# The expert stage of a one-core conv, attention and mixture-of-experts block: 39 groups of 256 slots against 32 groups of 256 and seven of 128

## The reference

```python
x = x + conv(group_norm(x))                 # 16 Fourier modes
t = tokens(x)
t = t + attention(layer_norm(t))            # causal within each sequence of 256
# mixture of experts, on layer_norm(t):
router_probs = softmax(flat_x @ router_w)   # 8 experts
topk_w, topk_idx = top_k(router_probs, 2)   # then normalised to sum 1
for e in range(8):
    h = gelu(flat_x @ w_fc[e])              # 256 -> 1024
    out = out + combine[:, e:e+1] * (h @ w_proj[e])   # 1024 -> 256
```

## Time and profile before

| | |
|---|---|
| median of 3 runs | 723.77 us (722.03 to 724.03) |
| the profiled execution | 726.27 us |
| its span, first to last instruction | 724.5 us |
| mean granted TensorE clock | 0.964 of full |
| busy: PE, DVE, ACT, POOL | 647.4, 516.5, 413.7, 429.6 us |
| instructions | 16522 |

### The profile page before, as it was taken

How to read it: one execution, slowest core, us unless ns; L and a number is a source line. 1 busy time by engine, 2 the same in 40 slices (tenths; PEclk the granted TensorE clock), 3 DMA queues, 4 the chain that set the end, 5 groups by cost and what they waited for, 6 DMA issues and landing times. The chain is left out here.

```text
span 724.5 us, 16522 instructions
## 1 busy us (share of the span) xinstructions
PE 647.4 (89%) x5010; PEld 624.2 (86%) x5010; DVE 516.5 (71%) x1217; ACT 413.7 (57%) x703; POOL 429.6 (59%) x340
## 2 busy tenths in 40 slices
PE   0496999999940699999999999999999999999993
PEld 0385888888840599999999999999999999999993
DVE  8764577777764577787878777877787777777761
ACT  1804777766520556566666656565656565756550
POOL 5002326777666256766666666767676767676763
PEclk9999999999975799999999999999999999999998
DMA  8805752222323454433131313222222222232312
GB/s 343 273 0 186 276 179 74 92 90 97 106 105 113 136 162 146 96 108 59 29 59 31 57 31 57 41 47 45 43 49 39 51 37 52 36 53 35 57 19 29
DMA packets 39486, 64.13 MB, mean 89 GB/s; under 512 B 3808, under 2 KB 34848, under 8 KB 38304
## 3 DMA queue, kind: packets, MB, share of 16 engines
q0 software_dynamic: 14304, 18.92, 14.7%
q1 hardware_dynamic: 14816, 34.55, 13.5%
q10 hardware_dynamic: 10336, 10.31, 5.6%
HBM read 37.96 MB, written 25.81 MB: 88 GB/s over the span
## 5 line engine op out<-in xcount | busy, mean ns | idle before, releaser
L574 POOL TENSOR_TENSOR pj_lo<-w_ffn,pj_hi 128x1024 fp32r<-128x1024 f32 x78 | 189.1, 2425 | 122.8 <-ACT pj_hi L615 106.3
L1167 DVE TENSOR_TENSOR fc_lo<-w_ffn,fc_hi 128x1024 fp32r<-128x1024 f32 x78 | 116.1, 1527 | 86.2 <-ACT fc_hi L615 86.2
L564 POOL DMA_INDIRECT out<-y,add_id x78 | 121.9, 1563 | 45.1 <-issue 43.7
L615 ACT ACTIVATE pj_hi<-w_ffn 128x1024 fp32r x78 | 82.7, 1060 | 94.9 <-PE psO L1464 89.3
L615 ACT ACTIVATE fc_hi<-w_ffn 128x1024 fp32r x78 | 78.3, 1051 | 43.4 <-issue 43.4
L1464 PE MATMUL psP<-pj_hi,h_hi 128*128 128x256 f32 x312 | 91.5, 293 | 0.2 <-DVE h_lo L1167 0.2
L1464 PE MATMUL psP<-pj_hi,h_lo 128*128 128x256 f32 x312 | 88.5, 284 | 0.0
L1464 PE MATMUL psO<-pj_hi,h_lo 128*128 128x256 f32 x312 | 88.3, 283 | 0.0
L1464 PE MATMUL psO<-pj_lo,h_hi 128*128 128x256 f32 x312 | 88.3, 283 | 0.0
L1464 PE MATMUL psP<-pj_lo,h_hi 128*128 128x256 f32 x312 | 88.3, 283 | 0.0
L1464 PE MATMUL psO<-pj_hi,h_hi 128*128 128x256 f32 x312 | 88.1, 282 | 0.0
(11 more groups left out here) (252 smaller groups left out, 1639.4 us busy)
## 6 DMA issues: line engine op xcount, KB each, us to landing
w_ffn<-in_w_ffn SPq DMA_DIRECT2D x8, 2048.0 KB, 8.2
xg<-slots ACTq DMA_DIRECT2D x38, 265.0 KB
xc<-in_x_ch SPq DMA_DIRECT2D x4, 1024.0 KB, 8.9
out<-x SPq DMA_DIRECT2D x16, 256.0 KB
x<-in_x_tok SPq DMA_DIRECT2D x1, 3072.0 KB, 25.2
slots<-fill SPq DMA_DIRECT2D x9, 265.0 KB, 2.8
out<-y,add_id POOLq DMA_INDIRECT x78, 3.9
w_in<-in_w_in SPq DMA_DIRECT2D x1, 1024.0 KB, 13.7
```

Of the source, the lines that this page charges most:

```text
L564: nc.gpsimd.indirect_dma_start(out_d, bass.IndirectOffsetOnAxis(ap=add_id[:, s:s + 1], axis=0), y[:, s, :], None, compute_op=ALU.add).then ...
L574: nc.gpsimd.tensor_tensor(pj_lo[:, 4 * a:4 * a + 4, :], w_ffn[:, bass.ds(e, 1), (2 + a) * DFF:(3 + a) * DFF].rearrange("p a (c d) -> p (a ...
L615: nc.scalar.activation(out, src, ACT.Copy, **kw).then_inc(done, 1)
L1167: v.tensor_tensor(out, whole, upper.bitcast(F32), ALU.subtract).then_inc(done, 1)
```

## The change

The groups are now of two sizes, 32 of 256 slots and seven of 128. In units of 128 slots the stage handles 2 x 32 + 7 = 71 where it handled 2 x 39 = 78. The number of groups stays 39.

- **The plan.** DVE gives each expert as many full groups as its count of picks divided by 256, rounded (the last one rounded up), 32 at most, and what is left of each goes to groups of 128. `plan_halves` works the latter out: 30 more DVE instructions in a chain of their own (`half_step`), placed after the planning chain and ahead of `after_attention`.
- **The order.** `PARTS` gives the sizes: six full groups, then three turns of a loop of ten positions (128, 256, 256, 256, 256, twice), then 128, 256, 256. The groups of 128 stand at positions 6, 11, 16, 21, 26, 31 and 36. All engines, POOL too, run through `run_groups`.
- **A group of 128.** `up` keeps its 48 matmuls with 128 moving columns; `down` has 24 with 256 columns; two transposes; the GELUs, casts and subtractions of hidden values have half the columns; one output and one indirect DMA. The splits of the weights (`fc_hi`, `fc_lo`, `pj_hi`, `pj_lo`) stay whole.
- **Two buffers.** `y` and `add_id` are double. `outputs(g)` waits for the adds of group g-2; `add(g)` copies the numbers first and waits for the adds of g-1 after that.
- Small tiles (`numbers`, `counts`, `past`, `plan`) move to other places in SBUF, and a helper `planned` has each engine wait for the second plan at position 4.

The core of the diff:

```diff
-GROUPS = (TOK * PICKS - E) // GS + E
+UNIT = GS // 2
+UNITS = (TOK * PICKS - E) // UNIT + E
+FULL = TOK * PICKS // GS
+HALVES = UNITS - 2 * FULL
+GROUPS = FULL + HALVES
+assert HALVES >= E - 1
+
+HEAD, ROUNDS = 6, 3
+ROUND = (1, 2, 2, 2, 2) * 2
+PARTS = (2,) * HEAD + ROUND * ROUNDS + (1, 2, 2)
+assert PARTS.count(2) == FULL and PARTS.count(1) == HALVES
...
+def group_of(n, turn=None):
+
+    parts = PARTS[n]
+    at = PARTS[:n].count(2) if parts == 2 else FULL + PARTS[:n].count(1)
+    added, added_last = (16 * sum(PARTS[:max(m, 0)]) for m in (n, n - 1))
+    if turn is None:
+        return Group(n, at, parts, added, added_last)
+    step = 16 * sum(ROUND)
+    return Group(turn * len(ROUND) + n, turn * ROUND.count(parts) + at, parts, turn * step + added, turn * step + added_last)
...
-        add_id = place("always", "add_id", [P, 2], I32)
+        add_id = [place("always", f"add_id{n}", [P, 2], I32) for n in range(2)]
...
-        y = ff("y", [P, 2, D])
+        y = [ff(f"y{n}", [P, 2, D]) for n in range(2)]
...
+        def planned(eng, g):
+
+            if isinstance(g.n, int) and g.n == HEAD - 2:
+                eng.wait_ge(halves_ready, 1)
+
         def load_group(eng, g):
-            at_row = eng.value_load(table[0:1, 1, bass.ds(g, 1)], min_val=0, max_val=IDLE_ROW)
-            eng.dma_start(xg[:, :, :], slots_d[bass.ds(at_row, GS)].rearrange("(s p) r -> p s r", p=P)).then_inc(xg_loaded, 16)
+            at_row = eng.value_load(table[0:1, 1, bass.ds(g.at, 1)], min_val=0, max_val=IDLE_ROW)
+            eng.dma_start(xg[:, 0:g.parts, :],
+                          slots_d[bass.ds(at_row, g.parts * P)].rearrange("(s p) r -> p s r", p=P)).then_inc(xg_loaded, 16)
...
+        def hidden_in(g, c):
+
+            return banks[c][:, :].rearrange("p (f n) -> p f n", f=2)[:, :, 0:g.parts * P]
 
         def run_groups(eng, body):
 
-            body(0, 0)
-            pairs = (GROUPS - 2) // 2
-            with eng.Fori(0, pairs) as i:
-                body(i * 2 + 1, 1)
-                body(i * 2 + 2, 0)
-            for g in range(1 + 2 * pairs, GROUPS):
-                body(g, g % 2)
+            def run(n, turn=None):
+
+                before, here, after, second = (
+                    group_of(m, turn) if turn is not None or 0 <= m < GROUPS else None for m in (n - 1, n, n + 1, n + 2))
+                body(before, here, after, second, n % 2)
+
+            for n in range(HEAD):
+                run(n)
...
+            for n in range(HEAD + len(ROUND) * ROUNDS, GROUPS):
+                run(n)
...
-            def add(g):
-                if later(g):
-                    pool.wait_ge(y_added, g * 32)
-                pool.wait_ge(meta_read, g * 2 + 2)
+            def add(g, par):
+                pool.wait_ge(meta_read, g.n * 2 + 2)
                 gate()
-                nc.gpsimd.tensor_copy(add_id[:, :], slot_id[:, bass.ds(g, 1), :]).then_inc(id_ready, 1)
-                pool.wait_ge(y_ready, g * 2 + 2)
-                pool.wait_ge(id_ready, g + 1)
+                nc.gpsimd.tensor_copy(add_id[par][:, 0:g.parts], slot_id[:, bass.ds(g.at, 1), 0:g.parts]).then_inc(id_ready, 1)
+                if later(g.n):
+                    pool.wait_ge(y_added, g.added)
+                pool.wait_ge(y_ready, g.n * 2 + 2)
+                pool.wait_ge(id_ready, g.n + 1)
                 gate()
-                for s in range(2):
+                for s in range(g.parts):
                     nc.gpsimd.indirect_dma_start(
-                        out_d, bass.IndirectOffsetOnAxis(ap=add_id[:, s:s + 1], axis=0), y[:, s, :], None,
+                        out_d, bass.IndirectOffsetOnAxis(ap=add_id[par][:, s:s + 1], axis=0), y[par][:, s, :], None,
                         compute_op=ALU.add).then_inc(y_added, 16)
...
+            def pool_group(before, g, after, second, par):
+
+                planned(pool, g)
+                if after is not None:
+                    proj_lower(after)
+                add(g, par)
...
-            def outputs(g):
-                act.wait_ge(down_mm, g * 2 + 2)
-                if later(g):
-                    act.wait_ge(y_added, g * 32)
-                for s, bank in enumerate((psP, psO)):
-                    nc.scalar.activation(y[:, s, :], bank[:, 0:D], ACT.Copy,
-                                         scale=slot_w[:, bass.ds(g, 1), s]).then_inc(y_ready, 1)
-
-            def act_group(g, par):
-                if g_on(g + 1):
-                    fc_upper(g + 1, 1 - par)
+                act.wait_ge(up_mm, g.n * 4 + c + 1)
+                h = hidden_in(g, c)
+                nc.scalar.activation(h, h, ACT.Gelu).then_inc(gelu_done, 1)
+
+            def outputs(g, par):
+                act.wait_ge(down_mm, g.n * 2 + 2)
+                if not isinstance(g.n, int) or g.n > 1:
+                    act.wait_ge(y_added, g.added_last)
+                for s, bank in enumerate((psP, psO)[:g.parts]):
+                    nc.scalar.activation(y[par][:, s, :], bank[:, 0:D], ACT.Copy,
+                                         scale=slot_w[:, bass.ds(g.at, 1), s]).then_inc(y_ready, 2 // g.parts)
...
-            step(v.tensor_scalar(n_groups, n_slots, 1.0 / GS, 127.5 / GS, ALU.mult, ALU.add))
+            v.tensor_scalar(n_groups[:, 0:E - 1], n_slots[:, 0:E - 1], 1.0 / GS, -0.5 / GS, ALU.mult, ALU.add)
+            step(v.tensor_scalar(n_groups[:, E - 1:E], n_slots[:, E - 1:E], 1.0 / GS, 127.5 / GS, ALU.mult, ALU.add))
             step(v.tensor_scalar(n_groups, n_groups, MAGIC, None, ALU.add))
             step(v.tensor_scalar(n_groups, n_groups, MAGIC, None, ALU.subtract))
-            step(v.tensor_tensor_scan(ends, ones, n_groups, 0.0, ALU.mult, ALU.add))
+            step(v.tensor_tensor_scan(whole, ones, n_groups, 0.0, ALU.mult, ALU.add))
+            step(v.tensor_scalar(ends, whole, float(FULL), None, ALU.min))
...
+            half_steps = [0]
+
+            def half(ins):
+                half_steps[0] += 1
+                ins.then_inc(half_step, 1)
+                dve.wait_ge(half_step, half_steps[0])
+
+            units, twice, left, half_ends = (half_units[:, n] for n in range(4))
+
+            def plan_halves():
+
+                half(v.tensor_scalar(units, n_slots, 1.0 / UNIT, 63.5 / UNIT, ALU.mult, ALU.add))
+                half(v.tensor_scalar(units, units, MAGIC, None, ALU.add))
+                half(v.tensor_scalar(units, units, MAGIC, None, ALU.subtract))
+                half(v.tensor_scalar(twice[:, 0:1], ends[:, 0:1], 2.0, None, ALU.mult))
+                half(v.tensor_tensor(twice[:, 1:E], ends[:, 1:E], ends[:, 0:E - 1], ALU.subtract))
+                half(v.tensor_scalar(twice[:, 1:E], twice[:, 1:E], 2.0, None, ALU.mult))
+                half(v.tensor_tensor(left, units, twice, ALU.subtract))
+                half(v.tensor_scalar(left, left, 0.0, None, ALU.max))
+                half(v.tensor_tensor_scan(half_ends, ones, left, 0.0, ALU.mult, ALU.add))
+                half(v.tensor_tensor(left, left, half_ends, ALU.subtract))
+                half(v.tensor_tensor(left, left, twice, ALU.add))
+                at_half = numbers[:, 0:HALVES, :]
+                past_h, next_h, base_h = (half_past[:, n] for n in range(3))
+                expert, row, real, weights_of, landed = (half_plan[:, n] for n in range(5))
+                half(v.tensor_tensor(past_h, at_half, half_ends.unsqueeze(1).broadcast_to([P, HALVES, E]), ALU.is_ge))
...
+                half(v.tensor_scalar(real, expert, float(E), float(UNIT), ALU.is_lt, ALU.mult))
+                half(v.tensor_tensor(row, row, real, ALU.mult))
...
+                half(v.tensor_scalar(landed, expert, 16.0, 16.0, ALU.mult, ALU.add))
+                v.tensor_copy(table[:, 2, FULL:GROUPS], landed).then_inc(halves_ready, 1)
...
+            def dve_group(before, g, after, second, par):
+                planned(dve, g)
+                if after is not None:
+                    fc_lower(after, 1 - par, expert_of(after))
                 hidden(g, 0)
...
+            plan_halves()
 
             after_attention(dve)
             dve.sem_inc(dve_passed, 1)
...
-                    for s in range(2):
+                    for s in range(g.parts):
...
-                            ins = mm(banks[c][:, (f % 2) * GS:(f % 2 + 1) * GS], w[:, hh, f * P:(f + 1) * P], m[:, hh, :],
+                            ins = mm(hidden_in(g, c)[:, f % 2, :], w[:, hh, f * P:(f + 1) * P], m[:, hh, 0:g.parts * P],
...
-                    for s, bank in enumerate((psP, psO)):
+                        pe.wait_ge(h_ready, g.n * 4 + f // 2 + 1)
+                    for s, bank in enumerate((psP, psO)[:g.parts]):
```

More of the change, by code:

```diff
@@ L1 @@
 from contextlib import ExitStack
+from dataclasses import dataclass
+from typing import Any
 import numpy as np
@@ L260, in hybrid_block @@
         behind_f = at("behind_f", [P, LATE - 1])
-        counts = at("counts", [P, 4, E])
+        counts = place("always", "counts", [P, 5, E])
         tail_f = at("tail_f", [P, E])
```

(69 more changed lines are left out.)

151 lines of the change are left out of this document (87 added, 64 removed).

## The result

The change is slower: 740.2 us (median of 4, 738.5 to 742.3) against 722.9 us (median of 4), a ratio of 1.0245 with a 95% interval of 1.0224 to 1.0266. The forecast of 707 and its range of 700 to 722 both missed. The profiled execution took 742.3 us with a span of 740.4; its mean granted clock is 0.934, against 0.964.

What follows compares the result with a forecast made beforehand. PE's own instruction list was taken to bound the expert stage. Short groups -22.7, second plan +7.8, start -1.6 and two buffers -0.5 gave -17.0 us, hence 707 us, with a range of 700 to 722.

Steps and rivals of the forecast that it cites:

- What bounds the kernel: Expert stage: it lasts as long as PE's own instructions; PE busy for 463.8 of 465.7 us.
- PE's side of a short group: Groups of 128 on PE: `up` matmuls at 0.105 us each, 8.2 us per group in place of 11.95.
- The rival of slow short matmuls: `up` with 128 columns runs slower than before, 10.6 us per group, total 742 us; chance 0.14.
- The same groups: the other engines: Short groups beside DVE, POOL and ACT: 8.5 us each plus 0.2 us of stall, 22.7 us less for seven.
- The rival of the tight ring: Unshortened weight splits of three engines make each short group cost 10.3 us in all, total 718 us; chance 0.09.
- The long loop: Rival at the loop's two jumps back: instruction waits add +3 to +6 us, total about 711 us; chance 0.05.
- The second plan: 30 new DVE steps ahead of the expert stage: 7.8 us more, bounds 6 and 20 us.
- The start: Load of group 1 hidden because the first `up` moves to about 250 us: 1.6 us less.
- Two buffers: Double output buffers at the stage's end, so the last output and DMA start earlier: 0.5 us less.

Runs made afterwards that it cites:

- experiment 1: The change with all 39 groups written out, no loop, order of sizes kept: 735.7 us, ratio 1.0185 to the kernel before.
- experiment 4: The kernel before, 39 full groups, with a loop of three turns of ten groups on PE, ACT and DVE: 732.3 us, ratio 1.0133.
- experiment 5: The kernel before, unchanged, traced a second time for its planning chain: 722.0 us in one execution.
- experiment 2: The change with ACT's `fc_hi` copies for group g+2 moved to the end of group g: 715.8 us, ratio 0.9888 to the kernel before.
- experiment 3: The change with POOL's `pj_lo` subtractions cut to 64 columns in full groups behind short ones, leaving out computation: 711.9 us, ratio 0.9863.
- experiment 6: The change with the seven groups of 128 last, behind 32 full ones, and a loop of two: 708.4 us, ratio 0.9819.
- experiment 7: The change with no loop, all groups written out, and ACT's `fc_hi` copies made early: 701.9 us, ratio 0.9710 to the kernel before.

## Why the prediction was wrong

**What bounds the kernel** was right: PE's list and the waits on it set the time, and the ledger adds up to the spans within 0.1 us.

**PE's side of a short group** was right: 8.2 us were worked out, 8.5 taken, 8.64 measured; a matmul of `up` takes 0.11 us against the assumed 0.105. The rival of slow short matmuls falls, though its 742 lies next to the result: that is luck, and a total that fits shows nothing by itself.

**The step that failed** is "The same groups: the other engines", in its last term: 0.2 us of stall for each full group behind a short one. It saw that `fc_hi` would come late, put that at 1 us, and set it against 2 us of slack in the other engines' timeline. Three things were wrong there. ACT is 2.0 us late against `up`, not 1. The slack was read off with an `fc_lo` of 3.2 us, as if that were the price of the work; the same trace had 1.2 to 2.6 for a single one, which asks for a reason, and the reason is POOL: moved by 2 us, `fc_lo` meets `pj_lo` along its whole length and takes 6.5. And each stall was priced by its length alone, where PE's half clock behind it adds 1.7 to 2.6 us. 0.2 became 5.2 to 6.2, 27 us for five groups (and 37 for seven, in experiment 1). The rival of the tight ring came nearest to the mechanism, a full group that needs the weight splits on time, but not in size: it gave a short group and its stall 10.3 us together, 1.8 more than the 8.5, a third of what the stalls took.

**The long loop** was priced at +3 to +6 for two jumps, with a chance of 0.05. Experiment 4 shows 3.9 and 4.2 each on full groups, and the change's own ledger 9.0 each, since the first group after the jump is a short one at half clock. The stall of PE itself, 2.0 us, is near the 1.7 from which it was worked out; again the clock was left out. It deserved more than 0.05, as nothing in the trace spoke against it. The section Instruction fetch mechanics of the Trainium skill, Runtime: NRT & Kernel Launch, was cited; experiment 4 agrees with the stall that it describes, with 2.1 and 2.4 us of PE.

**The second plan**: 6.5 us where 7.8 was taken, the low bound of 6 being nearer. The pace of the six wider steps (0.50) was drawn from a slow planning chain that was that execution's own, and width had nothing to do with it (experiment 5).

**The start**: the load of group 1 is hidden, 1.6 us, as said, but not because the first `up` came at about 250. It came at 240.4, for the first plan was fast, and the load was issued at 243.04 in place of 248.82. With a fast first plan and no second one the first `up` starts at 235.2 and 237.5 us (experiments 5 and 4), but PE then waits 3.0 and 2.4 us for this load, and group 1 begins at 253.9 and 255.7. With the second plan ahead of the stage it begins at 254.6 to 257.6 (the change, experiments 1 to 3, 6 and 7). So plan and load together cost some 1 to 2 us, where the forecast had 7.8 - 1.6 = 6.2.

**Two buffers**: 0.5 us at the end; the tail got 1.2 us shorter, which no experiment divides.

Had the other engines kept up and the loop cost nothing, the time would have been inside the range: experiment 7, the change without these two costs, gained 20.4 us by the medians against the 17.0 of the forecast. Part of that is two errors that cancel: over the groups it gained 20.9 in place of 22.7, and the start cost less than was priced.

## What to carry to other kernels

When an edit shortens a step on the bounding engine by 2 or 3 us, lay the other engines' timelines against the new start times and look at which instructions come to lie side by side, not only at how much slack each engine has. An instruction whose durations differ by a factor of two in one trace may have a partner that slows it, as here; look for it before trusting its mean. Price a stall of PE with the half clock behind it, which here, where the clock fell behind a stall of 2 to 4 us, added 40 to 85% of its length (three times and more behind a jump in front of a short group), and a long loop body by each jump back.

## What was not expected of the hardware

- A subtraction on DVE with both inputs in SBUF (128 x 1024) takes 1.21 to 1.27 us where it starts ahead of POOL's subtractions and up to 3.53 beside them, nearly a whole `pj_lo` of 2.4 us on top; one that reads PSUM keeps its 0.69 (128 x 512).
- A jump back over a body of ten groups (794 rows on PE and 420 on ACT in the change) stops PE for 2.0 to 2.4 us, ACT for 3.7 to 4.4 and DVE, which waits for ACT, for 5.4 to 6.1 (the change, experiments 3 and 4); over the body of 170 and 88 rows PE never waited, and ACT at most 1.0 us.
- Behind such a jump PE was granted half clock for 13.6 us while it was always busy, in a group with 128 moving columns in `up` (five of six such groups; in the sixth the clock did not fall); with 256 columns for 3.4 us.
